# Cross-attention and experts: router logits from extra matrix columns, all score banks exponentiated from PSUM, value and key-matrix products in turns

## The reference

```python
# block 1: the context asks nothing; the tokens (normalised x) are the queries
q = layernorm(norm(x)) @ Wq ; k, v = split(layernorm(context) @ Wkv)     # 16 heads of 64
q = q * (1 + side) + side                                                # side: per head and batch
x = x + softmax(q k^T / 8) v @ Wout
# block 2: each token goes to 2 of 9 experts
y = norm(x)
w, idx = top_2(softmax(y @ Wr)); w = w / sum(w)
x = x + sum over the two of w * (silu(y @ Wg[e]) * (y @ Wu[e])) @ Wd[e]
```

## Time and profile before

| engine | busy us | share of the span | instructions |
|---|---|---|---|
| PE | 859.2 | 91% | 6633 |
| DVE | 699.5 | 74% | 1638 |
| ACT | 652.2 | 69% | 2054 |
| POOL | 388.5 | 41% | 475 |

### The profile page before, as it was taken

How to read it: one execution, slowest core, us unless ns; L and a number is a source line. 1 busy time by engine, 2 the same in 40 slices (tenths; PEclk the granted TensorE clock), 3 DMA queues, 4 the chain that set the end, 5 groups by cost and what they waited for, 6 DMA issues and landing times.

```text
span 940.9 us, 22213 instructions
## 1 busy us (share of the span) xinstructions
PE 859.2 (91%) x6633; PEld 829.4 (88%) x6633; DVE 699.5 (74%) x1638; ACT 652.2 (69%) x2054; POOL 388.5 (41%) x475
## 2 busy tenths in 40 slices
PE   3968999999999998439999999999999999999993
PEld 3736899999999998429999999999999999999993
DVE  5647888888888777567777787867777777787771
ACT  3437888788788887236777677767777767677761
POOL 3000366777677666511334233433333333234332
PEclk9969999999999999759999999999999999999997
DMA  7167400401310204451223425254352253422222
GB/s 238 33 168 237 122 13 35 128 29 36 122 36 24 79 34 153 155 144 24 46 45 76 97 45 128 45 135 124 54 129 44 45 134 82 97 45 36 42 33 23
DMA packets 67877, 78.02 MB, mean 83 GB/s; under 512 B 8507, under 2 KB 59887, under 8 KB 67823
## 3 DMA queue, kind: packets, MB, share of 16 engines
q1 hardware_dynamic: 51055, 55.27, 20.2%
q0 software_dynamic: 14592, 18.95, 12.2%
q10 hardware_dynamic: 2176, 3.15, 1.1%
HBM read 113.49 MB, written 32.93 MB: 156 GB/s over the span
## 4 chain that ended last, share of the span: by engine, by line
PE 60%; DMA 12%; issue 8%; DVE 6%; ACT 5%; SPq 5%; POOL 3%; DVEq 1%; ACTq 0%; POOLq 0%
PE banks L225 17%; PE banks L227 17%; PE banks L226 16%; DMA wgt<-in_L_ffn_Wu 5%; DMA result<-res,tok_id 3%; PE banks L976 3%; PE banks L960 2%; DMA valmat_dram<-val_st 2%; ACT prob L748 2%; PE banks L1079 1%; PE banks L1046 1%; DVE hid_lo L1422 1%; DMA wr_sb<-in_L_ffn_Wr 1%; DVE prob_t_lo L1241 1%; PE banks L1000 1%
## 5 line engine op out<-in xcount | busy, mean ns | idle before, releaser
L225 PE MATMUL banks<-tok_t_hi,wgt_hi 128*128 128x256 f32 x880 | 251.1, 285 | 7.9 <-DVE tok_t_lo L1391 7.8
L226 PE MATMUL banks<-tok_t_lo,wgt_hi 128*128 128x256 f32 x880 | 250.1, 284 | 0.0
L227 PE MATMUL banks<-tok_t_hi,wgt_lo 128*128 128x256 f32 x880 | 250.1, 284 | 0.0
L1403 DVE TENSOR_TENSOR wgt_lo<-wgt,wgt_hi 128x704 fp32r<-128x704 f32 (+1 forms) x240 | 207.7, 908 | 36.4 <-ACT wgt_hi L808 35.1
L643 POOL DMA_INDIRECT result<-res,tok_id x80 | 129.1, 1614 | 214.9 <-ACT res L835 188.0
L808 ACT ACTIVATE wgt_hi<-wgt 128x704 fp32r (+3 forms) x240 | 179.9, 800 | 29.6 <-DMA wgt<-in_L_ffn_Wu 22.8
L225 PEld LDWEIGHTS banks<-tok_t_hi,wgt_hi 128*128 128x128 f32 x880 | 170.1, 193 | 9.8 <-issue 9.7
L226 PEld LDWEIGHTS banks<-tok_t_lo,wgt_hi 128*128 128x128 f32 x880 | 170.1, 193 | 0.0
L227 PEld LDWEIGHTS banks<-tok_t_hi,wgt_lo 128*128 128x128 f32 x880 | 170.1, 193 | 0.0
L225 PE MATMUL banks<-wgt_hi,hid_hi 128*128 128x256 f32 x400 | 116.2, 290 | 0.0
L227 PE MATMUL banks<-wgt_hi,hid_lo 128*128 128x256 f32 x400 | 113.1, 283 | 0.0
(11 more groups left out here) (175 smaller groups left out, 2103.1 us busy)
## 6 DMA issues: line engine op xcount, KB each, us to landing
wgt<-in_L_ffn_Wg SPq DMA_DIRECT2D x40, 704.0 KB
wgt<-in_L_ffn_Wu SPq DMA_DIRECT2D x40, 640.0 KB
wgt<-in_L_ffn_Wd SPq DMA_DIRECT2D x40, 640.0 KB
tok<-expert_in SPq DMA_DIRECT2D x40, 258.0 KB
wgt<-in_L_ffn_Wd SPq DMA_DIRECT2D x80, 64.0 KB
valmat_f<-valmat_dram SPq DMA_DIRECT2D x4, 1152.0 KB
xs<-in_x SPq DMA_DIRECT2D x4, 1024.0 KB, 9.5
expert_in<-blank SPq DMA_DIRECT2D x13, 258.0 KB, 9.5
```

Source lines behind the costliest of these rows:

```text
L225: nc.tensor.matmul(to, a[0], b[0], start=first, stop=False)
L226: nc.tensor.matmul(to, a[0], b[1], start=False, stop=False)
L227: return nc.tensor.matmul(to, a[1], b[0], start=False, stop=last)
L1403: nc.vector.tensor_tensor(wgt_lo[i][0:rows, p0:p1], loaded_weights(slot)[0:rows, p0:p1], wgt_hi[i][0:rows, p0:p1].bitcast(F32), ALU.subtra ...
```

## The change

In words:

1. The router's weights `wr` become 10 extra columns (`EX`: 9 experts and a zero column). They stand behind the last head in the key matrix (`HKE` = 1242 columns), so that the product of tile zn with it also gives zn by wr in bank 2; and Wout's rows get 10 more columns, Wout times wr, so that the value matrix has 266 columns (`DE`) and the value product also gives the attention's part of the logits in bank 6. From the two, the deviation of x (`x_dev`), its mean (`x_lack`) and y's mean, DVE puts the logits together (`own_logits`, `lacks`, `all_logits`); the factor of y's normalisation is put into the gate's exponential as its scale. PE's logits product, the transposes of xn and their move go.
2. In preparation PE turns Wout (16 transposes, before the first products), and makes the 18 small products of Wout and of a matrix of ones with wr (`PREP_WR`).
3. All three banks of scores are exponentiated by ACT from PSUM in the tile's own step, each behind its own minimum (`softmax_exp(s, c, i)`); `softmax_in` goes. `softmax_inv(s-1)` now waits for all three banks of tile s-1 and stands first in DVE's step.
4. Routing is one step earlier (`route` in the step of `add_attention`), so that the loop has one step less.
5. Value product m and key product m are made in turns: values in banks 0 to 3, keys in banks 4 to 7.
6. `wout_sb` and `v_t` lie in the last part of `xs`; `wout` is loaded ahead of `wq`.

The diff, cut to its core:

```diff
@@ constants, places
+EX = E + 1
+HKE = HK + EX
+DE = D + EX
-    valmat_dram = nc.dram_tensor("valmat_dram", (B, H, M, D), F32).ap()
+    valmat_dram = nc.dram_tensor("valmat_dram", (B, H, M, DE), F32).ap()
-        LAST_BANKS = (6, 7, 3)
+        LAST_BANKS = (3, 6, 7)
-            return bank[m % 8 if m < TURN_AT else LAST_BANKS[m - TURN_AT]]
+            return bank[4 + m % 4 if m < TURN_AT else LAST_BANKS[m - TURN_AT]]
-            return banks[:, 2 * (m % 4):2 * (m % 4) + 2, 0:D]
+            return banks[:, 2 * (m % 2):2 * (m % 2) + 2, 0:DE]
...
@@ SP
+            sp.dma_start(wout_sb[:, :, 0:D], wout.rearrange("(c p) n -> p c n", p=P)).then_inc(wout_loaded, 16)
             sp.dma_start(wq_sb[:], wq.rearrange("(k p) n -> p k n", p=P)).then_inc(wq_loaded, 16)
-            sp.dma_start(wout_sb[:], wout.rearrange("(c p) n -> p c n", p=P)).then_inc(wout_loaded, 16)
@@ POOL
-                if has(s, 5):
-                    make_rows(s - 5, c - 5)
+                if has(s, 4):
+                    make_rows(s - 4, c - 4)
...
@@ ACT, preparation
+            for n in range(4):
+                act.wait_ge(wout_turned, n + 1)
+                half = slice(n % 2 * INNER // 2, (n % 2 + 1) * INNER // 2)
+                nc.scalar.activation(wout_t[:, n // 2, half], bank[4 + n], ACT.Copy).then_inc(wout_moved, 1)
             round_kv(range(2, len(KV_PIECES)))
...
+            act.wait_ge(prep_made, PREP)
+            nc.scalar.activation(wout_sb[:, :, D:], prep_bank(PREP_WR)[:, 0:PAIRS * EX].rearrange("p (c n) -> p c n", c=PAIRS), ACT.Copy)
...
             for m in range(MATS):
...
+                if m < VALS and m % 2 == 0:
+                    val_move(m)
                 act.wait_ge(mat_made, m + 1)
@@ ACT, the loop
+            def softmax_exp(t, c, i):
+
+                act.wait_ge(row_min_made, t * len(SCORE_BANKS) + i + 1)
+                h0, h1 = SCORE_BANKS[i]
                 for h in range(h0, h1):
+                    ins = nc.scalar.activation(prob[c % 2][:, h * M:(h + 1) * M], bank[i][:, (h - h0) * M:(h - h0 + 1) * M],
+                                               ACT.Exp, bias=row_min[c % 2][:, h:h + 1], scale=-1.0,
+                                               accum_out=row_sum[c % 2][:, h:h + 1])
+                ins.then_inc(exp_done, 1)
...
-                if has(s, 1):
-                    softmax_exp(s - 1, c - 1, 0, SCORE_BANKS[DIRECT][0]).then_inc(exp_done, 1)
+                if has(s, 0):
+                    softmax_exp(s, c, 0)
                 if has(s, 2):
                     prob_round(s - 2, c - 2, NG - 1)
-                if turns(s):
+                if has(s, 0):
+                    softmax_exp(s, c, 1)
+                if has(s, -1):
                     turn_move(s, c)
+                if has(s, 3):
+                    act.wait_ge(gap_ready, s - 2)
+                    act.wait_ge(y_rstd_made, s - 2)
+                    nc.scalar.activation(gap_exp[(c - 3) % 2][:], gap[(c - 3) % 2][:], ACT.Exp, scale=y_rstd[:]).then_inc(gap_exp_done, 1)
...
                 if has(s, 0):
-                    softmax_direct(s, c)
+                    softmax_exp(s, c, 2)
@@ PE, preparation
+            pe.wait_ge(wout_loaded, 16)
+            for n in range(4):
+                for c in range(4):
+                    at = n % 2 * 4 + c
+                    mm = nc.tensor.transpose(bank[4 + n][:, c * P:(c + 1) * P], wout_sb[:, at, n // 2 * P:(n // 2 + 1) * P], ident[:])
+                mm.then_inc(wout_turned, 1)
+
             pe.wait_ge(ctx_split, 1)
+            pe.wait_ge(wout_moved, 4)
...
+            to = fill(PREP_WR)
+            for c in range(PAIRS + 1):
+                for k in range(KT):
+                    w = wout_t[:, k, c * P:(c + 1) * P] if c < PAIRS else ones[:]
+                    mm = nc.tensor.matmul(to[:, c * EX:(c + 1) * EX], w, wr_sb[:, k, :], start=k == 0, stop=k == KT - 1)
+            mm.then_inc(prep_made, 1)
...
+                if m < VALS:
+                    val(m)
+                if m >= 4:
+                    pe.wait_ge(mat_lo, m - 3)
@@ PE, the loop
-                if has(s, 4):
-                    pe.wait_ge(turn_moved, s + 1)
...
-                        mm = nc.tensor.matmul(bank[7][:, 0:E], xn_t[c % 2][:, k, :], wr_sb[:, k, :],
-                                              start=k == 0, stop=k == KT - 1)
-                    mm.then_inc(logits_done, 1)
...
-                            pe.wait_ge(direct_exp_done, (s - 1) * (len(SCORE_BANKS) - DIRECT) + i - DIRECT + 1)
+                            pe.wait_ge(exp_done, (s - 1) * len(SCORE_BANKS) + i + 1)
...
-            for s in range(T + 5):
+            for s in range(T + 4):
@@ DVE, the loop
             def softmax_inv(t, c):
-                dve.wait_ge(exp_done, t + 1)
+                dve.wait_ge(exp_done, (t + 1) * len(SCORE_BANKS))
                 nc.vector.reciprocal(row_inv[c % 2][:], row_sum[c % 2][:]).then_inc(inv_done, 1)
 
+            def all_logits(t, c):
+
+                settle()
+                nc.vector.scalar_tensor_tensor(out=centre[:], in0=wr_sum[:, 0:E], scalar=y_mv[:, 0:1], in1=x_logits[c % 4][:],
+                                               op0=ALU.mult, op1=ALU.subtract)
+                settle()
+                nc.vector.tensor_tensor(logits[:], bank[6][:, D:D + E], centre[:], ALU.subtract).then_inc(att_added, 1)
...
             def step(s, c):
+                if has(s, 1):
+                    softmax_inv(s - 1, c - 1)
+                if has(s, 4):
+                    dve.wait_ge(gate_den_made, s - 3)
+                    nc.vector.reciprocal(xn[(c - 4) % 4][:, 0, GATE:GATE + 1], gate_den[(c - 4) % 2][:]).then_inc(gate_made, 1)
+                    allot(s - 4, c - 4)
                 if has(s, 3):
                     add_attention(s - 3)
                 if has(s, 2):
+                    prob_rest(s - 2, c - 2, 0)
+                if has(s, 0):
+                    softmax_min(s, c, 0)
                 if has(s, 3):
+                    all_logits(s - 3, c - 3)
+                if has(s, 2):
+                    prob_rest(s - 2, c - 2, 1)
+                if has(s, 3):
+                    top_two(c - 3)
+                if has(s, 0):
+                    softmax_min(s, c, 1)
+                if has(s, 2):
+                    prob_rest(s - 2, c - 2, 2)
+                if has(s, 0):
+                    own_logits(s, c)
+                    softmax_min(s, c, 2)
+                if has(s, 3):
+                    route()
                     normalise(s - 3, c - 3)
```

More of the change, by code:

```diff
@@ L185, in program @@
         early.close()
[L186 removed]
+        val_st = [sb(f"val_st{i}", [P, STORE_HEADS, DE], F32, prep) for i in range(STORE_BUFFERS)]
         prep.close()
@@ L379, in has @@
             return 0 <= s - lag < T
-        def turns(s):
-            return has(s, -1) or has(s, 3)
         def turned_chunks(c0, c1):
@@ L1016, in step @@
                     turn_probs(s - 2, c - 2, NG - 1)
-                if turns(s):
+                if has(s, -1):
                     turn(s, c)
-                if has(s, 4):
-                    pe.wait_ge(picks_ready, s - 3)
-                    nc.tensor.matmul(bank[7][:, 16:16 + E], before[:], picks[:], start=True, stop=False)
-                    nc.tensor.matmul(bank[7][:, 16:16 + E], ones_h[:], picks_sum[:], start=False, stop=True
-                                     ).then_inc(ranks_done, 1)
                 if has(s, 2):
@@ L1031, in step @@
                     mm.then_inc(att_done, 1)
-            for s in range(T + 5):
+                if has(s, 3):
+                    pe.wait_ge(picks_ready, s - 2)
+                    nc.tensor.matmul(bank[7][:, 16:16 + E], before[:], picks[:], start=True, stop=False)
+                    nc.tensor.matmul(bank[7][:, 16:16 + E], ones_h[:], picks_sum[:], start=False, stop=True
+                                     ).then_inc(ranks_done, 1)
+            for s in range(T + 4):
                 step(s, s)
@@ L1247, in add_attention @@
                 row = xs[:, bass.ds(t * D, D)]
-                nc.vector.tensor_tensor(row, row, bank[6][:, 0:D], ALU.add).then_inc(att_added, 1)
+                nc.vector.tensor_tensor(row, row, bank[6][:, 0:D], ALU.add)
                 settle()
```

228 lines of the change are left out of this document (105 added, 123 removed).

## The result

The changed kernel takes 985.76 us (median of 4 runs, 983.12 to 988.66) against 942.59 us for the kernel before on the same chip (939.87 to 944.92): ratio 1.0466, 95% interval 1.0436 to 1.0495. I had forecast 947, with a range of 934 to 956. The change costs 43 us, and the forecast had the sign of the loop right and its size wrong.

The account below looks back on a forecast made before the run. TensorE bounds the loop before; after, a VectorE-ScalarE chain was to. Loop +9.8, preparation -2.5, tail -4.3 sum to +3.0 on 942.88, 945.9; 946.3 against the median, rounded up to 947 us, range 934 to 956.

Parts of the forecast that it names:

- part 2: Attention loop: a chain between VectorE and ScalarE replaces TensorE as the bound; 9.10 us a plain step, +9.8 us in all.
- `top_two` with two drains 0.65: VectorE's two best logits, between second remainder and bank 1's minimum: priced at 0.65 us of the loop's chain.
- the circle: Loop: VectorE's inverse waits for ScalarE's last exponentials, which wait for VectorE's minima; once round 9.10 us, above TensorE's 8.65.
- the loop's term: 27 steps x (9.10 - 9.07) plus 9.0 for three batches' value rounds and variances: +9.8 us.
- just under: POOL's own round in a loop step, about 8.7 us, was given no time of its own.
- part 3: Preparation: first store 8.2 us later, stores +1.3, 10.4 saved before the first scores; taken as -2.5 us.
- the cover of the value matrix behind the stores, 4 us: Loop's start: batch 0's value matrix lands about 4 us before its rounding, so later stores could hide there.
- The rival of the slow stores: Preparation: stores of 1,064-byte rows cost a fifth more, 40 us instead of 33.4; +5.4, 952 us; chance 0.14.
- Value rounds: Loop: `val_round` on ScalarE falls inside the chain in 12 of 32 steps; 2.5 us per batch, three times.
- both its signs: Loop: VectorE idle before the inverse until ScalarE's exponentials; ScalarE idle before its exponentials until the minima.
- the tail: Loop's end: one step less, last tile's routing 4.0 us instead of 8.5; -4.3 us.
- The clock did not fall: Rival: half of each of 12 value-round steps runs TensorE at 1.2 GHz; +35, 982 us; chance 0.04.

Follow-up runs that it names:

- Experiments 1 and 4: Two runs of the changed kernel: gap in tensor-scalar form, 964.12 us; and, separately, GpSimd dividing only head 0 of each tile, 960.32 us.
- experiment 5: Changed kernel with the first six of eight tiles of the second batch of x loaded ahead of the value matrix's stores: 979.04 us, ratio 1.0379.
- experiment 8: Changed kernel with preparation's products not in turns, all 24 value products first, then all 32 of the key matrix: 990.19 us, ratio 1.0502.
- experiment 9: Changed kernel with scalar gap, softmax_inv behind bank 0's minimum, early load of x, and VectorE's extra work spread over places with room: 942.04 us, ratio 0.9992.
- experiment 11: As experiment 9, with the first instruction of all_logits, centre, put ahead of the softmax inverse: 939.41 us, ratio 0.9938.

## Why the prediction was wrong

**The step that failed is `top_two` in part 2, "`top_two` with two drains 0.65".** The sum of the circle, 9.10 us, had `gap` in it at its 0.14 us, taken from a place where POOL was not dividing. In the new order the same instruction falls into the division. It measured 1.00, and 9.10 + 0.86 = 9.96 against 10.02; my upper bound for the step, 9.4, allowed only for dearer hand-offs. Experiments 1 and 4 take it out in two ways and land at 9.20 and 9.17, with a loop 21 and 24 us shorter. At 27 steps this is 23 of the 31.8 us that the loop's term missed; the wait for x is 6.4 more. I had written of POOL only that its own round was "just under"; I never asked what runs beside what. The kernel before shows the fault to who looks for it. At its loop's end a sum of nine numbers, 0.16 us in all other steps, is held to the end of the division (374.45 + 2.25 = 376.70):

```profile
374.70 2.02 DVE L1301 TENSOR_TENSOR picks_sum<-picks_sum,picks 128x9 f16<-128x9 f16 x1
```

```profile
374.45 2.25 POOL L604 TENSOR_TENSOR prob<-prob,row_inv 128x1232 f32<-128x1232 f32 x1 [0.94 <-DVE row_inv L1280]
```

The Trainium skill, SBUF — State Buffer, "Who interferes with whom", has the rule: VectorE with two inputs in SBUF and a GpSimd instruction that reads SBUF need the same second read port, and the one that comes later waits for the other's whole instruction. The traces agree: 1.00 and 2.35 us for `gap` and `centre`, ending with the division, while a remainder of 512 columns with one input in PSUM (275.84, 0.68 us) runs beside the division unharmed. It was the rule to weigh in the forecast, in the place of the one on descriptors.

**The wait for x, part 3.** I had counted the cover of the value matrix behind the stores, 4 us, and not that of the next load in the same queue, which VectorE wants earlier. 6.4 us in the profile; experiment 5 takes that wait away and wins 7 us, 4.2 of it in the loop's stage. Part 3 lists what the additions delay on TensorE's, ScalarE's and VectorE's queues, but not what stands behind the stores on SP's.

**Preparation, part 3.** First products where forecast (20.86 against 20.6). First store 51.7 against 49.5: the products of the router's columns are at 43.35 to 47.4, and the Wq products begin at 36.44 instead of 31.82. Then a pair of a value and a key product takes 1.36 us (starts 60.91 and 62.27), not 1.07: the key product costs 0.71 in turns, where two of its passes cost 0.58 in a block, and the value product 0.65. 24 pairs by 0.29 is 7 us, in part in place of waiting for stores, which no longer set the pace. Why turns make a product dearer, no run isolates. So +2.4 instead of -2.5. What turns save was right (10.8 against 10.4, experiment 8).

**Smaller errors of the working.** While the value products were made, TensorE was idle for 9.3 of 27.8 us, not for most of the time. It did not stand still for over 4 us around 94 us: its wait was 2.84 us (92.75 to 95.59), and with the 1.41 us in front of 88.86 it makes 4.25. The rival of the slow stores says that 4 us of cover come off first, but its 5.4 is without them; with them it is 1.4, and 948 instead of 952. Value rounds were not free before either: the steps of one were 0.4 to 0.6 us longer than four plain ones.

**What was right.** The circle and both its signs; the value rounds (2.8 a batch longer than plain steps, 2.3 more than before, against 3.0); the tail, -4.8 against -4.3; TensorE's own work per step, 8.42 where its timeline has no wait (the last batch of experiment 9), against 8.65. Stores of 1,064 bytes were no hindrance: TensorE, not the stores, set the pace. The clock did not fall (0.969 against 0.964): as before, it was at its lower level only for a few us behind a long wait at the loop's start (0.50 from 106 to 110 us).

**Where the expected gain is.** With the faults out (experiment 11) the plain step is 8.56 instead of 9.07 and the tail 5.8 us shorter. But the first scores come 4.4 later in its profile, and the loop as a whole is only 1.8 shorter (280.4 against 282.2). Counted from score product to score product on TensorE, the plain steps win 6.1 us, the three value rounds lose 2.9 (their twelve steps take 113.3 against 110.4) and the first five steps 1.3. In a value round TensorE is busy for 35.6 of 37.8 us and waits for the remainder, and VectorE waits 2.1: neither is full, the chain between the engines holds the round. What is left is 0.6%.

## What to carry to other kernels

Before an instruction is moved to another place in the order, list for the new place what the neighbour engines run at that time, POOL's long SBUF instructions above all, and look whether any VectorE instruction with two SBUF operands falls into them; a mean per line can hide it (`centre` was held in one tile of 32 of the changed kernel), the longest duration of a line beside its median shows it. Put such instructions where a semaphore guarantees that the long one has not begun (ahead of what releases it), not where it happens not to have. And when a wait is put in front of a queue, of engine or DMA, price what stands second in it.

## What was not expected of the hardware

- A VectorE instruction of 128x1 took 0.14 us alone and up to 1.55 us beside POOL's 2.24 us division, ending with it each time it was held; in tensor-scalar form it took 0.19 us in the same place. Whether VectorE can hold up POOL in the same way is not seen in these traces: the division stayed at 2.24 to 2.26 us, also where `centre` is recorded ahead of it and is held.
- FIND_INDEX8, which also names two tensors in SBUF, was never held: 0.16 us in all 32 steps (159 to 164 ns), at 276.93 in the middle of the division. It may be no exception: the same line leaves a MATCH_VALUE_LOAD of 0.09 us just ahead of it (276.85), so each of the two may read one of the tensors. No run tells.
- Work in turns kept TensorE's granted clock at 1.00 in preparation where the same work in two blocks, waiting for store buffers, ran at 0.50 (60 to 70 us).
- The start of the loop varies by 2 to 5 us between kernels with the same preparation (84.9 to 87.2 us without the early load, 85.3 to 90.7 with it), which is as much as the later experiments differ by. What causes it stays open.
